# A graph network kernel on one core: float32r parts in place of bfloat16 parts, with widened edge counts

## The reference

```
h = relu(layernorm(x))
for l in 1, 2, 3:                       # SAGE layers, relu behind the first two
    h = (segment_sum(h[src], dst) / count) @ Wl.T + b + h @ Wr.T
x = x + h
h = relu(layernorm(x))
messages = gelu((h[src] + edge_attr) @ We1 + be1) @ We2 + be2
u = (1 + eps) * h + segment_sum(messages, dst)
out = x + gelu(u @ Wu1 + bu1) @ Wu2 + bu2
```

## Time and profile before

| | |
|---|---|
| median of 3 runs | 1129.02 us (1119.06 to 1130.83) |
| the profiled execution | 1121.82 us, of which the span is 1119.4 us |
| PE busy | 988.1 us, 88% of the span |
| POOL busy | 375.2 us |
| DVE busy | 506.0 us |
| granted TensorE clock, mean | 0.931 |

### The profile page before, as it was taken

How to read it: one execution, slowest core, us unless ns; L and a number is a source line. 1 busy time by engine, 2 the same in 40 slices (tenths; PEclk the granted TensorE clock), 3 DMA queues, 4 the chain that set the end, 5 groups by cost and what they waited for, 6 DMA issues and landing times.

```text
span 1119.4 us, 16242 instructions
## 1 busy us (share of the span) xinstructions
PE 988.1 (88%) x5619; PEld 604.1 (54%) x5619; DVE 506.0 (45%) x1984; ACT 256.2 (23%) x449; POOL 375.2 (34%) x394
## 2 busy tenths in 40 slices
PE   5879999999999999974967898897899789899896
PEld 2544555554445445541655565564576466556564
DVE  7799999841112111142733343343335244344342
ACT  3666777711011101010111011011011011101111
POOL 1000000000000112165855465645636655665650
PEclk9889999999999999986978899898879989999997
DMA  3200100010000000063332233333233333333330
GB/s 125 51 2 12 12 11 12 12 56 1 1 1 1 10 10 19 10 121 105 100 87 79 81 108 81 97 97 95 82 82 106 82 93 99 83 109 83 92 92 17
DMA packets 47474, 67.60 MB, mean 60 GB/s; under 512 B 15745, under 2 KB 26204, under 8 KB 47260
## 3 DMA queue, kind: packets, MB, share of 16 engines
q1 hardware_dynamic: 35996, 43.16, 14.3%
q0 software_dynamic: 11392, 23.35, 8.1%
HBM read 63.18 MB, written 3.30 MB: 59 GB/s over the span
## 4 chain that ended last, share of the span: by engine, by line
PE 75%; DVE 11%; issue 7%; another core or an unknown queue 4%; ACT 1%; DMA 1%; SPq 0%; ACTq 0%; DVEq 0%
PE f_ps L1193 22%; PE f_ps L1247 22%; PE f_ps L1309 10%; PE f_ps L1233 7%; DVE f_region L616 2%; DVE f_region L614 2%; PE f_ps L1078 2%; DVE f_region L620 1%; DVE f_region L618 1%; PE f_ps L1071 1%; PE f_ps L1168 1%; PE f_ps L1229 1%; PE f_ps L1130 1%; PE f_ps L1255 1%
## 5 line engine op out<-in xcount | busy, mean ns | idle before, releaser
L564 POOL DMA_INDIRECT f_adj<-table,f_table_idx x356 | 353.7, 994 | 251.5 <-DVE f_adj L914 151.9
L1193 PE MATMUL f_ps<-f_adj,f_parts 125*128 125x500 fp8e4 (+1 forms) x1575 | 331.5, 352 | 0.1
L1247 PE MATMUL f_ps<-f_parts 125*128 125x512 bf16 x1125 | 276.4, 396 | 30.5 <-issue 25.5
L1193 PEld LDWEIGHTS f_ps<-f_adj,f_parts 125*128 125x128 bf16 x1575 | 143.5, 97 | 129.9 <-issue 11.1
L1247 PEld LDWEIGHTS f_ps<-f_parts 125*128 125x128 bf16 x1125 | 113.2, 101 | 181.1 <-issue 72.2
L1309 PE MATMUL f_ps<-f_adj 128*128 128x94 f32 (+20 forms) x984 | 141.4, 287 | 42.3 <-issue 32.5
L806 DVE TENSOR_SCALAR f_parts<-f_parts 128x512 bf16<-128x512 f16 x375 | 94.0, 297 | 170.4 <-PE f_ps L1247 93.9
L1309 PEld LDWEIGHTS f_ps<-f_adj 128*128 128x128 f32 x984 | 138.5, 208 | 59.1 <-issue 46.2
L549 POOL TENSOR_TENSOR f_rest<-f_region,f_parts 125x512 f32<-125x512 f32 (+1 forms) x7 | 7.3, 1050 | 462.6 <-ACT f_parts L1033 462.6
L945 ACT CAST f_adj<-f_ps 128x500 f32 x213 | 126.1, 592 | 56.5 <-PE f_ps L1078 40.6
L786 DVE TENSOR_SCALAR f_adj<-f_iota,f_dst_abs 128x94 f32<-128x94 f16 (+4 forms) x416 | 85.6, 273 | 112.4 <-remote 62.8
(11 more groups left out here) (140 smaller groups left out, 532.9 us busy)
## 6 DMA issues: line engine op xcount, KB each, us to landing
f_region<-in_edge_attr_T SPq DMA_DIRECT2D x103, 256.0 KB
f_adj<-table,f_table_idx POOLq DMA_INDIRECT x356
f_parts<-in_src_row SPq DMA_DIRECT2D x15, 256.0 KB
f_adj<-inv SPq DMA_DIRECT2D x1, 1562.5 KB
table<-f_region SPq DMA_DIRECT2D x6, 250.0 KB
out<-f_xT SPq DMA_DIRECT2D x6, 250.0 KB
f_rcntT<-inv SPq DMA_DIRECT2D x5, 250.0 KB, 3.9
f_xT<-in_xT SPq DMA_DIRECT2D x1, 812.5 KB, 5.8
```

What stands on the lines that cost most here:

```text
L564: pool.indirect_dma_start(out=rows[:, r % RW, j * D:(j + 1) * D], out_offset=None, in_=table, in_offset=bass.IndirectOffsetOnAxis(ap=table ...
L1193: ins = pe.matmul(ps[:, dense_ps(i):dense_ps(i) + width(c)], parts[0:NP, (l % 2) * 3 + p, b, :], adj[0:NP, b, lo:hi].bitcast(F8), start=b ...
L1247: ins = pe.matmul(z_columns(g), parts[0:NP, 3 + p, b, :], select[0:NP, u % SELECT, :], start=b == 0 and p == 0, stop=b == NB - 1 and p == ...
```

## The change

The second and the third layer use two parts of type float32r in place of three of bfloat16. The high part is a copy by ACT into a float32r tensor, the other is the remainder, by one DVE instruction; `split_mid` and `split_low` remain for the first layer alone, which stays as it is with three bfloat16 parts (`PARTS = (3, 2, 2)`). In these matmuls the moving operand is float32r as well: each 125x500 piece of `adj` is first widened from bytes to float32r into a ring of five tiles (`wide`). Each piece is used by two matmuls. Of every five tiles DVE makes two, ACT two and POOL one (`TURNS`), and a tile is made anew when PE has signalled that the one before it in the ring is spent. The last chunk streams 126 columns. `Plan` puts the widening of a slot's pieces one slot ahead (`expand`). `AFTER` goes from 9 to 8.

The table rows are split into two float32r parts, by ACT and one POOL instruction, and a selection takes 25 blocks times 2 parts. The one-hots of the selections are float32r, in a ring of 8. Twelve groups are picked in place of 15, so 93 are gathered in place of 90 (the last one is a single tile). The memory is laid out anew: the ring `wide` lies over the edge feature buffers, so the first five are read only once the last dense unit is done. The check of the counts (one reduction over 3,125 columns) is spread over seven slots.

```diff
-        self.SHARES = 15
+        self.SHARES = 12
...
-    PARTS = 3
+    PARTS = (3, 2, 2)
     RATE = 2.3
-    AFTER = 9
+    AFTER = 8
...
+        self.after = min(slot for slot, units in self.units.items() if units[-1][0] >= s.NC)
...
+        for slot, units in self.units.items():
+            for n, b, i in units:
+                if n >= s.NC and i == 0:
+                    assert slot >= s.GB
+                    self.put("expand", slot - 1, (n, b))
...
-        later = slot + 6 if slot < self.GB else slot
         self.put("turn", slot, k)
         self.put("high", slot, k)
         self.put("rest", self.dve(slot), k)
-        self.put("mid", later, k)
-        self.put("low", self.dve(later), k)
 
...
+    WIDE, NEXTS = 5, 3
     AHEAD, OH_AHEAD = 2, 2
-    SELECT = 12
+    SELECT = 8
...
+        PAIR = 2 * NB * D * 4
+        second, third = slab("second", PAIR), slab("third", PAIR)
+        pair = [None, placed_at("pair2", [P, 2, NB, D], F32R, second), placed_at("pair3", [P, 2, NB, D], F32R, third)]
+        x_rows = placed_at("x_rows", [P, NB, D], F32, second)
+        chosen = pair[1]
+        parts1 = placed_at("parts1", [P, 3, NB, D], BF16, third)
...
+        wide = placed_at("wide", [P, WIDE, CHUNK], F32R, by_slot)
...
+        ON_DVE, ON_ACT, ON_POOL = range(3)
+        TURNS = (ON_DVE, ON_ACT, ON_DVE, ON_ACT, ON_POOL)
+
+        def owner(u):
+            return TURNS[u % WIDE]
+
+        def wide_count(u):
+            return sum(owner(v) == owner(u) for v in range(u + 1))
+
+        def wide_tile(u):
+            return wide[0:NP, u % WIDE, 0:streamed((u // NB) % NC)]
+
+        def bytes_of(u):
+            lo = s.cols((u // NB) % NC)[0]
+            return adj[0:NP, u % NB, lo:lo + streamed((u // NB) % NC)]
+
+        def wait_spent(engine, u):
+            if u % NB == NB - 1:
+                engine.wait_ge(dense_done, NC + u // NB + 1)
+            else:
+                engine.wait_ge(spent, u + 1 - u // NB)
+
+        def streamed(c):
+            return width(c) + width(c) % 2
+
+        def ordinal(n, b):
+            return (n - NC) * NB + b
 
         def t_rows(c):
...
+                if c == NC - 1:
+                    sp.wait_ge(dense_done, LAYERS * NC)
+                    for g in range(EA):
+                        sp.dma_start(ea[:, g, 0:s.tiles(g) * P], edge_columns(g)).then_inc(ea_in[g], 16)
...
-            for c in range(NC):
-                part3 = [part(1, i, c) for i in range(3)]
+
+            def split3(c):
                 pool.wait_ge(high3, c + 1)
-                pool.tensor_tensor(rest3_rows(c), grow_rows(c), part3[0], ALU.subtract).then_inc(rest3, 1)
-                pool.wait_ge(rest3, c + 1)
-                pool.tensor_copy(part3[1], rest3_rows(c)).then_inc(mid3, 1)
-                pool.wait_ge(mid3, c + 1)
-                pool.tensor_tensor(part3[2], rest3_rows(c), part3[1], ALU.subtract).then_inc(lowest3, 1)
+                pool.tensor_tensor(part(chosen, 1, c), grow_rows(c), part(chosen, 0, c).bitcast(F32), ALU.subtract
+                                   ).then_inc(lowest3, 1)
+
+            pool.wait_ge(summed, GB)
+            pool.wait_ge(kept, GB)
+            for n in range(NC, LAYERS * NC):
+                c = n - 2 * NC - 1
+                for b in range(NB):
+                    u = ordinal(n, b)
+                    if owner(u) != ON_POOL:
+                        continue
+                    if u >= WIDE:
+                        wait_spent(pool, u - WIDE)
+                    pool.tensor_copy(wide_tile(u), bytes_of(u)).then_inc(widened[ON_POOL], 1)
+                    if 0 <= c < NC - 2 and b // WIDE == 2:
+                        split3(c)
+            for c in range(NC - 2, NC):
+                split3(c)
             pool.wait_ge(rows_out[0], 16 * ((NC + 1) // 2))
             pool.wait_ge(rows_out[1], 16 * (NC // 2))
             pool.wait_ge(tile_in, 32)
...
+                    dve.tensor_tensor(part(pair[l], 1, c), t_rows(c), part(pair[l], 0, c).bitcast(F32),
+                                      ALU.subtract).then_inc(lowest, 1)
...
+            def widen_dve(u):
+                if u == 0:
+                    dve.wait_ge(summed, GB)
+                    dve.wait_ge(kept, GB)
+                if u >= WIDE:
+                    wait_spent(dve, u - WIDE)
+                dve.tensor_copy(wide_tile(u), bytes_of(u)).then_inc(widened[ON_DVE], 1)
...
+                for n, b in plan.due("expand", slot):
+                    if owner(ordinal(n, b)) == ON_DVE:
+                        widen_dve(ordinal(n, b))
...
-                ins = pe.matmul(ps[:, dense_ps(i):dense_ps(i) + width(c)], parts[0:NP, (l % 2) * 3 + p, b, :],
-                                adj[0:NP, b, lo:hi].bitcast(F8), start=b == 0 and p == 0,
-                                stop=b == NB - 1 and p == 2)
-                if b == NB - 1 and p == 2:
+                if l == 0:
+                    ins = pe.matmul(ps[:, dense_ps(i):dense_ps(i) + width(c)], parts1[0:NP, p, b, :],
+                                    adj[0:NP, b, lo:hi].bitcast(F8), start=b == 0 and p == 0,
+                                    stop=b == NB - 1 and p == plan.PARTS[0] - 1)
+                else:
+                    u = ordinal(i, b)
+                    if p == 0:
+                        pe.wait_ge(widened[owner(u)], wide_count(u))
+                    ins = pe.matmul(ps[:, dense_ps(i):dense_ps(i) + streamed(c)], pair[l][0:NP, p, b, :], wide_tile(u),
+                                    start=b == 0 and p == 0, stop=b == NB - 1 and p == 1)
+                    if p == 1 and b < NB - 1:
+                        ins.then_inc(spent, 1)
+                if b == NB - 1 and p == plan.PARTS[l] - 1:
...
-                for p in range(3):
-                    ins = pe.matmul(z_columns(g), parts[0:NP, 3 + p, b, :], select[0:NP, u % SELECT, :],
-                                    start=b == 0 and p == 0, stop=b == NB - 1 and p == 2, skip_group_check=True)
+                for p in range(2):
+                    ins = pe.matmul(z_columns(g), chosen[0:NP, p, b, :], select[0:NP, u % SELECT, :],
+                                    start=b == 0 and p == 0, stop=b == NB - 1 and p == 1, skip_group_check=True)
                 ins.then_inc(selected, 1)
 
```

More of the change, by code:

```diff
@@ L11 @@
 F32 = mybir.dt.float32
+F32R = mybir.dt.float32r
 BF16 = mybir.dt.bfloat16
@@ L194, in dense @@
             for b in range(s.NB):
-                for i in range(self.PARTS):
+                for i in range(self.PARTS[n // s.NC]):
                     while budget >= (self.RATE if slot < s.GB else self.AFTER):
@@ L232, in fast_path @@
     EVEN = NP + NP % 2
-    CALM = GB + 8
+    CALM = [plan.after + 4 + 2 * c for c in range(NC)]
     KEYS = s.A_COLS + s.DW * NB - s.B_FROM
@@ L252, in fast_path, with slab, placed_at @@
         ps = ctx.enter_context(nc.psum_tensor("f_ps", [P, 8 * BANK], F32))
+        def slab(name, size):
+            base = -(-nc.sbuf_base // 32) * 32
+            sb(name, [P, size], U8)
+            assert nc.sbuf_base >= base + size
+            return base
+        def placed_at(name, shape, dt, offset):
+            k[name] = nc.alloc_sbuf_tensor_at("f_" + name, shape, dt, offset=offset)
+            return k[name]
         ident, mean, cent = sb("ident", [P, P]), sb("mean", [P, P]), sb("cent", [P, P])
@@ L393, in in_nodes, with part @@
             return a[lo:hi]
-        def part(l, i, c):
+        def part(of, i, c):
             b = s.blocks(c)
-            return parts[0:NP, (l % 2) * 3 + i, b[0]:b[-1] + 1, :].rearrange("p b d -> p (b d)")
+            return of[0:NP, i, b[0]:b[-1] + 1, :].rearrange("p b d -> p (b d)")
         def rest_rows(j):
-            return rest[0:NP, j % 2, 0:len(s.blocks(j % NC)) * D]
+            return rest1[0:NP, j % 2, 0:len(s.blocks(j % NC)) * D]
+        ON_DVE, ON_ACT, ON_POOL = range(3)
[18 more added lines that the diff above has]
+            return (n - NC) * NB + b
         def t_rows(c):
@@ L685, in mean_rows @@
                     dve.wait_ge(active, i - 1)
-                dve.tensor_tensor(work[:, i % 2, 0:width(c)], ps[:, dense_ps(i):dense_ps(i) + width(c)], at(rcntT, c),
-                                  ALU.mult).then_inc(agg_kept, 1)
+                sums = ps[:, dense_ps(i):dense_ps(i) + width(c)]
+                if i < NC:
+                    dve.tensor_tensor(work[:, i % 2, 0:width(c)], sums, at(rcntT, c), ALU.mult).then_inc(agg_kept, 1)
+                else:
+                    dve.scalar_tensor_tensor(out=work[:, i % 2, 0:width(c)], in0=sums, scalar=UNIT, in1=at(rcntT, c),
+                                             op0=ALU.mult, op1=ALU.mult).then_inc(agg_kept, 1)
             def join_own(i):
@@ L937, in _ @@
             act.wait_ge(eye, 4)
+            act.wait_ge(margin, 1)
             def keep_block(g):
@@ L984, in split_high, with widen_act @@
                 if l == 0:
```

(20 more changed lines are left out.)

100 lines of the change are left out of this document (53 added, 47 removed).

## The result

The changed kernel takes **1083.19 us** (median of 4 runs, 1076.99 to 1107.89) beside 1129.92 us of the kernel before (1119.06 to 1131.53) on the same chip: a ratio of 0.9588, 95% interval 0.9489 to 0.9686. One of the four runs (1107.89) counts as slow and isn't in the ratio. Forecast were 976 us, with a range of 928 to 1048. The profiled execution is 1078.62 us, its span 1076.9.

A forecast was written before the change was run, and what follows sets the result against it. PE was taken as the bound, with POOL some 20% below in the edge stage. First gather 486.6 - 66.3 + 18 + 4 = 442.3, plus 500, plus 25: span 967.3, execution 969.7, times 1.0064: 976 us; 80% range 928 to 1048.

The forecast's parts named there:

- I take 500 us from the first gather to the last: Edge stage: PE's and POOL's loads nearly tie, so 500 us in place of 603.5; bounds 478 and 554.
- Its first term: Edge stage, POOL: 368 gathers at 1.25 us are 460 us, plus 17 us beyond their usual time, 478 us.
- Its second: Edge stage: irregular waits between two queues with a ring of six groups lift 478 us to 500.
- Rival 4: Edge stage: PE's late instructions shrink with their number or vanish behind POOL, 930 or 938 us; chance 0.09.
- Matmuls: Dense stage: float32r streams at 0.211 us per 500 columns, 198.9 us become 132.6, minus 66.3; selections minus 113.4.
- rival 3: PE's matmuls: float32r streams more than once, 0.42 us per 500 columns, 1211 us in all; chance 0.09.
- the widening: Dense stage: casting tiles of bytes costs 1.3 us for each of 14 chunks, 18 us; bounds 0 and 42.
- rival 1: Dense stage: widening holds PE back throughout, 36 us more than taken, about 1012 us; chance 0.13.
- where 4 were forecast: Between dense and edge stage: first five edge blocks are read later, ahead of the ids, 4 us; bounds 0 and 10.
- Rival 2: Edge stage: DVE's busier stretches and longer one-hots slow POOL's gathers to 1.34 or 1.45 us, 995 to 1030; chance 0.09.
- The end: From the last gather's start to the span's end: 25 us in place of 29.3; bounds 18 and 29.3.
- -66.3 + 18 + 4 - 115: Dense matmuls saved, widening, reads between the stages, and PE's edge-stage saving (selections 113.4, fewer picked groups about 2), in us.

The follow-up runs named there:

- experiments 1 and 2: SP's plain transfers in place of POOL's indirect gathers: in the changed kernel 845.63 and 845.76 us, then in the kernel before 990.49 us.
- 5: 31 pauses put into POOL's gathers: changed kernel 1024.03 us (ratio 1.0454) and 1026.30 us (0.9235) on two kinds of chip; kernel before 1047.61 us (1.0684).
- 6: Changed kernel with POOL issuing its 368 transfers as plain ones of consecutive rows, not indirect: 841.77 us beside 1114.53 us of the kernel before.
- 3: Both kernels again, unaltered: changed 1090.82 us beside 1125.16 on one kind of chip, 934.52 beside 980.57 on the other; kernel before 1125.57 us.

## Why the prediction was wrong

**The step that failed** is the edge stage, "I take 500 us from the first gather to the last". Its first term was right: gathers and what they take beyond it were put at 478 us, and 606.7 less 126.8 us of waits are 479.9. Its second, 22 us for POOL's waits between two nearly equal loads, measured **126.8 us**. I took the 151.9 us of before as PE's work, to vanish with that work, and all 603.5 us as PE's load. They were not: without gathers the kernel before takes 124 us less in all, with PE busy for 426 of 428 us in the main part of the stage. The difference was PE's late instructions and the lower granted clock beside them (0.91 against 1.00), and these come with POOL's gathering, so they did not shrink as PE's work did. On B, where nothing comes late, the stage doesn't gain either (some 475 us, an estimate, and 475.7 now), because there POOL's own 368 gathers fill it: taking work from PE could bring the stage to POOL's load and no lower. Rival 4 had weighed these rows with the wrong sign, as going by the number of instructions or vanishing behind POOL.

**The rest held.** Matmuls: one stream each (rival 3 falls), but 0.0145 us dearer in 600 and 0.013 in 600, so 16.5 us short. The dense stage as a whole: first gather forecast at 442.3, measured 438.26. The first matmuls behind the last dense unit, before and now, are these:

```profile
477.67 1.03 PE L1114 MATMUL f_ps<-f_mean,f_region 128*125 128x1 f32 x8
...
424.06 0.98 PE L1215 MATMUL f_ps<-f_mean,f_by_edge 128*125 128x1 f32 x8
```

The dense units end 53.6 us earlier (66.3 less 18 forecast). With the matmuls 8.7 us dearer, some 4 us are left for the widening in place of 18: the ring covered nearly all, and PE waited about 1 us for casts of 500 columns; rival 1 falls. From there to the first gather are 14.2 us in place of 9.0, so 5 us more where 4 were forecast. The casts took 455 (DVE), 611 (ACT) and 627 ns (POOL) for 500 elements, within the bounds. DVE's 300 new one-hots took 430 ns on the mean, which is the estimate of 129 us for 300 that the prediction took from the Trainium skill ("VectorE: DVE Perf Modes", the perf-mode tier table), and 115.2 us busy, since they overlap; they were hidden as said. Rival 2 is small: 1.304 us for a gather and its pause on A, 1.293 on B. The end was 32.0 us on the A-chip in place of 25, and 16.0 on B.

PE's savings were sized well. The terms of the prediction, -66.3 + 18 + 4 - 115, corrected by 16.5, give -143 us; experiments 1 and 2 measured -144.7, good to some 10 us. On B the sum of parts, 442.3 + 500 + 25, stands against 436.7 + 475.7 + 16.0: 39 us too long. That 934.5 us lie inside the stated range is luck, since the time before is 980 there and the forecast started from 1129; the saving forecast was 153 us and is 46. Two slips in the prediction had no effect: in the build stage DVE was the fuller engine, not PE (201.8 against 196.8 us of 224), and rival 3's 1202 us give 1212 by the same factors, not 1211.

**Shown**: it is POOL's gathers (1, 2), breaks in them halve PE's late time and shorten the whole (5), bytes and PE's count are not the cause (1), the packets of POOL's queue alone neither (6), and only some chips have it (3). **Argued only**: that it is the loading of instructions that is late, as the expectations say. The profile says "issue" and "remote". Its queues from 559 to 575 us, around the stretch shown above, are no more than these (packets, MB, share):

```profile
q0 software_dynamic: 380, 0.77, 18.2%
q8 instruction: 1, 0.02, 0.4%
```

The DMA engines had room. The one block of instructions came between 574 and 575 us, when PE was back at its rate or nearly, and none from 559 to 574. So the trace shows no block on the DMA engines that PE could have waited for in those 14 us; what paced its instructions at 0.7 us stays open. Whether it needs the indirection or only POOL's work without a break stays open too, and so does what differs between the chips.

## What to carry to other kernels

Before a gain on one engine is counted, look at what its idle time was: small "issue" gaps that begin and end with another engine's run of work don't go away with less work. Two queues that throttle each other through a ring give back what one of them saves; exchange the suspect's operations for harmless ones of the same size first, and see what the stage takes without them. Take an engine's load in a stage from such a run, not from the stage's length. Compare only with a run of the old kernel on the same chip, since here one stage differed by 131 us between chips while the changed kernel's first gather came within 3 us on the three where it was traced as it is.

## What the runs showed of the hardware

Float32r operands stream at nearly the rate of narrower ones: 0.229 against 0.216 us for 512 columns (bfloat16), and 0.225 against 0.211 for 500 (bfloat16 against float8), all at a granted clock of 1.00. And an edge stage with 368 indirect gathers takes 131 us more on one kind of chip than on the other, at the same 1.25 us rhythm and with the same build and dense stages; without the gathers the kinds agree (845.63 and 845.76 us).
